# The decayed second factor U formed from the decayed Q on GpSimd, and one sum over an added pair of square halves on TensorE

## The reference, cut to what matters

```python
lora = jnp.tanh(x @ theta_w1) @ theta_w2
theta = jnp.clip(theta_base + lora, -THETA_CLIP, THETA_CLIP)
log_z = complex(-(lambda_base + viscosity_eta * theta ** 2) * dt, theta * dt)
cumlog = jnp.cumsum(log_z, axis=1)
A = where(mask, exp(cumlog[:, :, None] - cumlog[:, None, :]), 0)
S_intra = einsum('btshk,bshp->bthpk', A * bc[:, :, None], x_disc)
S_total = exp(cumlog)[..., None, :] * state[:, None] + S_intra
y = einsum('bthk,bthpk->bthp', cc, S_total).real
...
g = (y + x_ssm * D) * silu(z)
g = g * rsqrt(mean(g * g, axis=-1) + RMS_EPS) * norm_w
return g @ out_proj_w.T
```

## Time and profile before

| | us |
|---|---|
| median of three runs | 310.38 |
| lowest and highest run | 310.25, 310.92 |
| the profiled execution, its own time | 311.79 |
| span of the profiled execution | 309.9 |
| TensorE busy | 281.6 (91% of the span) |
| TensorE weight loads busy | 209.5 (68%) |
| VectorE busy | 256.5 (83%) |
| ScalarE busy | 189.9 (61%) |
| GpSimd busy | 194.4 (63%) |

### The profile page before, as it was taken

One profiled execution on the slowest core, in us unless ns is written; L12 is line 12 of the kernel. 1 busy time (PEld: TensorE's weight loads), 2 busy tenths in 40 slices (PEclk: granted clock), 3 DMA queues, 4 the chain that ended last, 5 costly groups with the idle time before them and its releaser, 6 DMA issues.

```text
span 309.9 us, 9434 instructions
## 1 busy us (share of the span) xinstructions
PE 281.6 (91%) x3899; PEld 209.5 (68%) x3899; DVE 256.5 (83%) x630; ACT 189.9 (61%) x351; POOL 194.4 (63%) x165
## 2 busy tenths in 40 slices
PE   1876896999999999999999999999999999978982
PEld 1643365787688768787587768776788767846772
DVE  4887995789889889988998989988998986998931
ACT  1876667487539865678538854787557853673210
POOL 2102799149990999359972999189945996199001
PEclk9989597999999999999999999999999999999998
DMA  7502300141112201230113202230114010320101
GB/s 178 148 0 62 76 0 2 44 95 37 34 39 70 68 2 37 72 87 19 34 36 88 52 3 60 62 87 2 35 25 100 19 34 4 78 61 0 37 4 42
DMA packets 19467, 15.00 MB, mean 48 GB/s; under 512 B 5109, under 2 KB 15194, under 8 KB 19418
## 3 DMA queue, kind: packets, MB, share of 16 engines
q1 hardware_dynamic: 17640, 13.96, 17.8%
q10 hardware_dynamic: 1778, 0.36, 0.6%
HBM read 3.83 MB, written 2.10 MB: 19 GB/s over the span
## 4 chain that ended last, share of the span: by engine, by line
PE 71%; DVE 16%; ACT 7%; issue 3%; DMA 1%; DVEq 0%; POOL 0%; POOLq 0%; ACTq 0%
PE bank L1585 10%; PE bank L1661 8%; PE bank L1662 8%; PE bank L1672 5%; PE bank L1682 5%; PE bank L1719 4%; PE bank L1712 4%; PE bank L1792 4%; PE bank L1763 4%; PE bank L1748 3%; PE bank L1692 3%; ACT z L1174 2%; PE bank L1650 2%; PE bank L1728 2%; PE bank L1651 2%
## 5 line engine op out<-in xcount | busy, mean ns | idle before, releaser
L1421 POOL TENSOR_TENSOR btmp<-cims,X 128x512 f32<-128x512 f32 x15 | 19.1, 1271 | 56.9 <-ACT X L1191 56.4
L1661 PE MATMUL bank<-h0h,W 128*128 128x512 f16 x128 | 50.1, 391 | 4.5 <-DVE h0l L865 4.5
L1662 PE MATMUL bank<-h0l,W 128*128 128x512 f16 x128 | 50.0, 391 | 0.0
L1585 PE MATMUL bank<-XW,xh 128*128 128x256 f16 x256 | 46.1, 277 | 1.1 <-ACT xh L1120 1.1
L1224 ACT ACTIVATE h1h<-bank 128x512 f16<-128x512 f32 x32 | 19.0, 593 | 27.2 <-PE bank L1662 27.2
L1585 PE MATMUL bank<-XW,xl 128*128 128x256 f16 x128 | 35.5, 280 | 0.0
L1585 PEld LDWEIGHTS bank<-XW,xh 128*128 128x128 f16 x256 | 25.2, 99 | 5.2 <-ACT xh L1120 1.4
L1180 ACT ACTIVATE tin<-bank,base 128x256 f32<-128x256 f32 x16 | 6.7, 470 | 34.6 <-PE bank L1635 34.6
L1661 PEld LDWEIGHTS bank<-h0h,W 128*128 128x128 f16 x128 | 13.9, 108 | 19.2 <-DVE h0l L865 5.0
L865 DVE SCALAR_TENSOR_TENSOR h1l<-bank,h1h 128x512 f16<-128x512 f32 x32 | 21.8, 685 | 3.9 <-ACT h1h L1224 3.2
L788 DVE TENSOR_TENSOR GT<-bank,const 128x512 f32<-128x512 f32 x32 | 19.9, 684 | 5.2 <-PE bank L1692 5.2
(11 more groups left out here) (207 smaller groups left out, 839.1 us busy)
## 6 DMA issues: line engine op xcount, KB each, us to landing
xtok<-in_x SPq DMA_DIRECT2D x8, 256.0 KB, 3.4
cims<-bc SPq DMA_DIRECT2D x32, 64.0 KB, 2.1
cres<-bc SPq DMA_DIRECT2D x32, 64.0 KB, 2.2
bres<-bc SPq DMA_DIRECT2D x32, 64.0 KB, 2.1
bims<-bc SPq DMA_DIRECT2D x32, 64.0 KB, 2.1
out<-osb SPq DMA_DIRECT2D x7, 256.0 KB, 2.3
const<-constants SPq DMA_DIRECT2D x1, 512.0 KB, 6.5
KT<-in_in_proj_w ACTq DMA_DIRECT2D x1, 320.0 KB, 4.4
```

The lines of the kernel that those rows point to most:

```text
L1421: P.tensor_tensor(btmp[1][:], b[:], f2, ALU.mult).then_inc(sig.sem, 1)
L1585: return M.matmul(bank[6 + half][:, INNER * (c % 2):INNER * (c % 2) + INNER], tok(x, c, k), w[:, k, :], start=start, stop=True, skip_group ...
L1661: M.matmul(banks[f][:], w, h0h[:, k, :], start=(k == 0), stop=False)
L1662: last = M.matmul(banks[f][:], w, h0l[:, k, :], start=False, stop=(k == MT - 1))
```

## The change

Four things change, in turns 1 to 6 alone where nothing else is said.

- GpSimd no longer multiplies B by R. After Bre it waits for Q and multiplies B by Q (`b_times_queries`), so that U comes out decayed. The six instructions stand behind the three of Bre instead of ahead of them; `rms_of` stands between U's halves as before.
- VectorE drops the last step of U (1024 columns). `decayed(n, 1, (0, 1), 2)` counts the two steps that it did, so that the sixth is reached with Q. TensorE waits for U at `g_products` by GpSimd's own count (`s_v`); SyncE, which repeats B's rows, waits for it as well.
- VectorE adds the two halves of `gsq` into `gsum` (`halves_added`) right behind K, and `mean_squares` moves behind `k_re_times_b`, which moves ahead of the dt steps.
- TensorE sums `gsum` (`sums_of_added`), four products in place of eight, in one piece behind `mlp1` tile 1; and `x_products(n+1, 1)` moves ahead of `dt_products(n+1)`.

```diff
-            def decayed(n, part, halves=(0, 1)):
+            def decayed(n, part, halves=(0, 1), closing=0):
...
-                                     view(growth, 0, 128, 0, [[0, count], [1, T]]), ALU.mult), linked=False, by=count)
+                                     view(growth, 0, 128, 0, [[0, count], [1, T]]), ALU.mult), linked=False, by=count + closing)
...
+            def halves_added(n):
+                v.wait_ge(a_gsq.sem, a_gsq.done(n))
+                V.tensor_tensor(gsum[:], gsq[:, 0, :], gsq[:, 1, :], ALU.add).then_inc(s_gsum, 1)
...
                 decayed(n, 0)
+                halves_added(n - 1)
+                h1_low(n, 0)
+                decayed(n, 1, (0, 1), 2)
+                h1_low(n, 1)
+                k_re_times_b(n)
                 mean_squares(n - 1)
-                h1_low(n, 0)
-                decayed(n, 1)
-                h1_low(n, 1)
                 dt_input(n + 1)
                 dt_steps(n + 1)
                 final(n - 1, pq, stored)
-                k_re_times_b(n)
                 h1_low(n, 2)
                 h1_low(n, 3)
-                decayed(n, 2)
                 bc_taps(n + 1)
                 add_mlp(n, n % XBUFS)
...
+            def b_times_queries(n, between):
+                g.wait_ge(s_kq.sem, s_kq.at(n, 4))
+                turned(s_v, n, Ure, Uim, ((bres, bims), (Q[:, 0, :], Q[:, 1, :])), between=between)
...
                     c_rotated(n)
-                    b_times_rotated(n, between=lambda: rms_of(n - 1))
                     b_and_k(n, s_kq, 0)
+                    b_times_queries(n, lambda: rms_of(n - 1))
                     b_and_k_rest(n)
...
+            def sums_of_added(n):
+                pe.wait_ge(s_gsum, n + 1)
+                for c in range(NCH):
+                    last = M.matmul(sums_in[:, c:c + 1], gsum[:, CH * c:CH * c + CH], all_ones(1), start=True, stop=True)
+                last.then_inc(t_ms.sem, 1)
...
                     pe.wait_ge(s_kq.sem, s_kq.done(b))
+                    pe.wait_ge(s_v.sem, s_v.done(b))
...
                     xn_transposed(n + 1, True)
+                if has_front:
+                    mlp1(n, (0, 1))
                 if has_back:
-                    sums_of_squares(b, (0, 1))
+                    sums_of_added(b)
                 if has_front:
-                    mlp1(n, (0,))
-                if has_back:
-                    sums_of_squares(b, (2, 3))
-                if has_front:
-                    mlp1(n, (1,))
                     if has_next:
+                        x_products(n + 1, 1)
                         dt_products(n + 1)
-                        x_products(n + 1, 1)
                         bc_products(n + 1)
                     mlp1(n, (2, 3))
```

More of the change, by code:

```diff
@@ L264, in build @@
         gsq = sb("gsq", [128, 2, T])
+        gsum = sb("gsum", [128, T])
         msq = sb("msq", [128, NCH])
@@ L319, in build @@
         s_msq = signal("mean_squares", 1)
+        s_gsum = sem("square_halves_added")
         s_bk = signal("B_K", 6)
@@ L482, in repeat_bc @@
                     sp.wait_ge(s_bk.sem, s_bk.at(n, 0))
+                    sp.wait_ge(s_v.sem, s_v.at(n, 0))
                 repeat_rows(0, bres, b_in)
```

## The result

The changed kernel takes 316.47 us (median of 4 runs, 314.95 to 317.44) against 310.31 (4 runs): a ratio of 1.0208, 95% interval 1.0175 to 1.0241. The forecast was 317.1. The profiled execution took 316.27 us with a span of 314.5.

The account below looks back on a forecast made before the run. TensorE was taken as the bound, busy 33.72 of 33.82 us a turn. Six turns x 1.2 us, less 0.5, added 6.7 us to the median of 310.38: 317.1 us, with an 8-in-10 range of 313.3 to 319.2.

Parts of the forecast that it names:

- The sums, first group: At `mlp1` tile 0 on TensorE: these sums were filling the wait for `h0l`, so removing them gives nothing.
- The sums, second group: Behind `mlp1` tile 1, TensorE waits for `gsum` before summing, making every turn 0.65 us longer.
- The collision of `tmpb`: VectorE's `tmpb` meets GpSimd's third Bre instruction, takes 1.5 to 1.6 us; `dt_products` starts 0.55 us after TensorE came.
- What that collision is worth: Rival without collision at `tmpb`: only the wait for `gsum` counts, 0.65 us a turn, 313.8 us; chance 0.19.
- GpSimd, "covered, by 0.5 us": GpSimd's chain from K to Bim ends at 193.3, before TensorE reaches `g_across` at 193.95: covered by 0.5 us.
- The forecast of 35.0: A turn, from one `g_across` to the next, should take 35.0 us after the change.
- VectorE, "priced at nothing": On VectorE, U's last step goes and `gsum` comes: some 0.55 us less work a turn, priced at nothing.
- the rival of a second delay: Collision hits GpSimd's following instruction too, or late `final` holds up `mlp_out`: turn 1.5 to 1.8 us longer; chance 0.12.
- `lora1`: TensorE no longer waits for U at `lora1`; 0.5 us goes away in the one long turn.
- The rival that TensorE keeps what it saves: At `mlp1` tile 1's end, timely `gsum` and no `mean_squares` hold-up gain 0.81 us a turn: 305.0 us; chance 0.05.
- no wait for `gsum` either: Lower bound on the two new TensorE waits: with neither, TensorE would keep its 0.81 us.
- The sum: Over six turns: 6 x 1.2 = 7.2, less 0.5 for the long turn: 6.7 us, giving 317.1 us.

Follow-up runs that it names:

- experiment 2: The changed kernel with `tmpb`'s second operand read from PSUM instead of SBUF (Bim then not the reference's): 316.20 us, ratio 1.0176 to the kernel before.
- experiment 1: The changed kernel with VectorE's `mean_squares` ahead of `tmpb` instead of behind it: 316.08 us, ratio 1.0189 to the kernel before.
- experiment 5: experiment 1 with `rms_of` on GpSimd between Bre and U instead of between U's halves: 316.02 us, ratio 1.0200 to the kernel before.
- experiment 10: U part alone, all sums and the mean squares moved ahead, `rms` in GpSimd's wait for K, `xd` behind the roots: 310.22 us, ratio 0.9996 to before.
- experiment 3: U part of the change alone, all sixteen products of the sums as before, no `gsum`: 314.87 us, ratio 1.0140 to the kernel before.
- Experiment 4: Sums part of the change alone, U as before the change: 327.54 us, ratio 1.0461 to the kernel before.
- experiment 7: The changed kernel with `halves_added` (`gsum`) ahead of K instead of behind it: 316.56 us, ratio 1.0211 to the kernel before.
- experiment 8: The changed kernel with `gsum` ahead of K, mean squares ahead of `tmpb` and this ahead of `final`, `rms` ahead of U: 314.54 us, ratio 1.0153 to before.
- Experiment 9: experiment 1 with GpSimd's `xd` behind the reciprocal roots of the next layernorm: 314.87 us, ratio 1.0162 to the kernel before.
- experiment 6: experiment 3 with `rms_of` between Bre and U: 311.86 us, ratio 1.0090 to the kernel before.

## Why the prediction was right, and where it was not

*The sums, first group.* Right: `mlp1` tile 0 waits 0.54 us for `h0l` where the sums stood, and starts 15.36 us behind `g_across`, against 15.40 before.

*The sums, second group.* Right in size and mechanism. Predicted 0.65 us a turn; `x_products` starts 20.33 us behind `g_across` in the first turn, where TensorE stood at 19.66 before with all its sums done: 0.67. TensorE's idle time there is shown as 0.50 us.

*The collision of `tmpb`.* The mechanism is shown by experiment 2 (1.58 us back to 0.68), and the size was forecast as 1.5 to 1.6. The dt products were to start 0.55 us after TensorE came to them; they start 0.47 us later than without the wait (23.42 behind `g_across` in the first turn, against 22.95 in experiment 1), of which 0.30 are shown as idle.

*What that collision is worth.* Here a step failed. The prediction read that without it only the wait for `gsum` would count, 0.65 us a turn. Experiment 1 removed the wait and had such a turn once, the first (34.50); from the second on it gained nothing (34.93). What the collision costs beside the wait is 0.33 us on GpSimd, through the loop (experiment 2: 34.60).

*GpSimd, "covered, by 0.5 us".* The chain itself was forecast within 0.02 us: Bim ends 16.82 us after K's start, predicted 16.83 (193.3 against 176.47). The cover at `g_across` is what was said, 195.69 against 195.18. But the step stopped at Bim. The next instruction in GpSimd's queue, `xd`, moved with it, from 15.13 to 16.89 us behind K, and VectorE's `vare` ends with it in every row of the table from after to experiment 5. That loop gives 34.93 us. TensorE's own path with its two waits gives 34.87, as the first turn of the change shows, in which the loop is not yet in force (`from_state` starts 8.98 us behind `g_across`, as before the change; in the later turns at 9.05, just when S is there). The forecast of 35.0 was right for TensorE's path, and it was luck that the loop, which it didn't see, lies only 0.07 us above.

*VectorE, "priced at nothing".* Its spared work is worth nothing, as said (experiment 10). That nothing on it would be late was wrong: in the loop VectorE goes from `vare` to S without idling, and experiments 1 and 3 show TensorE 0.37 us waiting for it. The dt steps start 2.4 us later than before, not 1.9 (23.96 against 21.58 behind `g_across`). The wait ahead of `mlp_out` was named in the rival of a second delay; it is 0.40 us in experiment 3, and not there in the change itself.

*`lora1`.* Right; the wait is gone. Experiment 4, with the old order of U, has it in every turn (0.8 to 1.4 us).

*The rival that TensorE keeps what it saves.* Its price of 305.0 us was wrong by the prediction's own rows: if the first group's time is taken by the wait for `h0l`, the second group is still to be done, and TensorE reaches 178.56 instead of 178.59. With `gsum` in time, experiments 7 and 8 have 0.09 us of gain there, not 0.81. So "no wait for `gsum` either" would have left TensorE next to nothing.

*The sum.* Six turns cost 6.15 us, forecast 6.7 (7.2 less 0.5). In the first turn it is 1.05 us: 0.67 for `gsum` and 0.47 for the mean squares, less 0.09 between `bc_products` and `lora1` (6.81 us, 6.90 before; perhaps a wait for U too short to be shown). The loop adds 0.07 in the others. Experiment 9 opened both, the loop and the wait for the mean squares, and is left with 0.67. What `xd` behind the roots would be worth by itself was not run; by these rows it would be 0.07 us a turn, an estimate, since TensorE's own path holds 34.87.

## What to carry to other kernels

When a chain on a secondary engine gets later, follow its queue one instruction beyond the last result that the main engine waits for: here the cover was right at `g_across`, and the loop closed through the instruction behind it. Look for tiny operations with a long duration (`vare`, 128x4 in 1.40 us): they mark two engines tied together without a semaphore, and no table of waits shows them. And when a removed wait comes back elsewhere at the same size, measure all engines from one common event, as in the table above; kernels whose intervals agree to 0.02 us give the loop away. Look at the first turn by itself, too: it shows what a turn takes before the loop is in force.

## What the runs showed of the hardware

- A VectorE operation with four elements a partition and no second tensor operand is held by GpSimd's work too: `vare` took 0.17 us alone and 0.68 (before), 1.40, 1.53, 1.70 and 1.87 us beside the 1.90 us `xd`, always until this ended; in experiment 8 it was held in the same way until Bim's last instruction ended (0.56 to 1.02 us). I had looked for it only in products with two SBUF operands, where it is 0.68 us against 1.43 and 1.51, and up to 1.68 in the experiments.
- It works both ways: GpSimd's first product behind K takes 1.35 us with `gsum` beside it and 1.06 without (experiment 3), and `rms` 1.35 instead of 1.02 where it meets `tmpb` (experiments 5 and 6).
- Eight instructions with one moving column take 0.8 to 0.9 us of TensorE, yet taking eight away made no version faster: half of the sums had filled the wait for `h0l`, and with `gsum` in time `x_products` started 0.09 us earlier (experiments 7 and 8).
- The granted clock fell to the lower level (0.50, 1.2 GHz) for 3.2 us behind a wait of 1.48 us in experiment 4, in one turn of six. The turns before and after it had waits of 1.47 and 1.48 us at the same place and kept 1.00.
